# A decoder layer's written order of events: fewer, longer runs of weighings

## What is computed

```python
def _attn(q_in, k_in, v_in, wq, bq, wk, bk, wv, bv, wo, bo, causal):
    Q = (q_in @ wq + bq).reshape(Bq, Sq, H, HD)
    Kp = (k_in @ wk + bk).reshape(Bq, Sk, H, HD)
    V = (v_in @ wv + bv).reshape(Bq, Sk, H, HD)
    scores = jnp.einsum('bqhd,bkhd->bhqk', Q, Kp) / jnp.sqrt(jnp.float32(HD))
    if causal:
        scores = jnp.where(mask, scores, -jnp.inf)
    a = jax.nn.softmax(scores, axis=-1)
    o = jnp.einsum('bhqk,bkhd->bqhd', a, V).reshape(Bq, Sq, Dm)
    return o @ wo + bo
x = _layernorm(x + _attn(x, x, x, sa_wq, sa_bq, sa_wk, sa_bk, sa_wv, sa_bv, sa_wo, sa_bo, True), ln1_g, ln1_b)
x = _layernorm(x + _attn(x, encoder_output, encoder_output, ca_wq, ca_bq, ca_wk, ca_bk, ca_wv, ca_bv, ca_wo, ca_bo, False), ln2_g, ln2_b)
x = _layernorm(x + _moe(x, router_w, router_b, e_w1, e_b1, e_w2, e_b2), ln3_g, ln3_b)
```

## Time and profile before

| | us |
|---|---|
| three runs | 981.31, 982.85, 984.86 |
| their median | 982.85 |
| the profiled execution | 977.55 |
| its span, first to last instruction | 975.8 |
| PE busy in the span | 943.1 |
| DVE busy | 593.7 |
| ACT busy | 557.3 |
| POOL busy | 341.0 |
| matmuls L946 (1,024 of cross, in the page's group) busy | 129.5 |

### The profile page before, as it was taken

How to read it: one execution, slowest core, us unless ns; L and a number is a source line. 1 busy time by engine, 2 the same in 40 slices (tenths; PEclk the granted TensorE clock), 3 DMA queues, 4 the chain that set the end, 5 groups by cost and what they waited for, 6 DMA issues and landing times.

```text
span 975.8 us, 18808 instructions
## 1 busy us (share of the span) xinstructions
PE 943.1 (97%) x5812; PEld 551.2 (56%) x5813; DVE 593.7 (61%) x1006; ACT 557.3 (57%) x1164; POOL 341.0 (35%) x465
## 2 busy tenths in 40 slices
PE   7899999999999999999999999998998999999995
PEld 4456543533445445333543334234898999999974
DVE  4657798788777887787787788863431211212226
ACT  3354566677765656777666766785343444444442
POOL 3465853534325435313446036112441111111115
PEclk9799999999999999999999999998999999999998
DMA  7363323213114111201624022002231344334225
GB/s 218 99 168 81 92 78 97 56 45 92 43 52 115 50 66 34 66 2 41 215 92 149 4 69 64 12 21 62 44 116 39 118 129 124 120 106 140 49 75 199
DMA packets 93899, 84.04 MB, mean 86 GB/s; under 512 B 37638, under 2 KB 87302, under 8 KB 93702
## 3 DMA queue, kind: packets, MB, share of 16 engines
q1 hardware_dynamic: 85436, 63.93, 23.6%
q0 software_dynamic: 5360, 16.82, 5.0%
q10 hardware_dynamic: 3040, 2.49, 1.0%
HBM read 38.63 MB, written 12.63 MB: 53 GB/s over the span
## 4 chain that ended last, share of the span: by engine, by line
PE 87%; PEld 3%; DVE 3%; DMA 2%; POOL 1%; issue 1%; ACT 1%; PEldq 0%; ACTq 0%; POOLq 0%; DVEq 0%
PE o_bank L946 16%; PE a_bank L929 16%; PE v_slot L893 11%; PE v_slot L1433 11%; PE a_bank L1427 9%; PE a_bank L858 6%; PE a_bank L876 4%; PE v_slot L897 4%; PE v_slot L957 3%; PE o_bank L1427 3%; PE v_slot L898 2%; PEld a_bank L1427 1%; DVE max_q L1116 1%; PEld v_slot L1433 1%; DMA b_sa_bk<-in_sa_bk 1%
## 5 line engine op out<-in xcount | busy, mean ns | idle before, releaser
L1062 ACT ACTIVATE probs<-a_bank 128x512 f32<-128x512 f32 (+1 forms) x688 | 360.3, 591 | 143.4 <-PE a_bank L929 138.0
L1116 DVE TENSOR_REDUCE max_q<-v_slot 128x1 f32<-128x1024 f32 (+3 forms) x352 | 397.8, 1169 | 69.6 <-PE v_slot L893 43.6
L929 PE MATMUL a_bank<-q_stack_cross,k_stack_cross 99*128 99x512 bf16 x512 | 162.8, 381 | 0.6 <-ACT probs L1062 0.3
L1439 ACT ACTIVATE hidden<-a_bank,b 128x128 f32<-128x128 f32 x216 | 79.1, 367 | 144.4 <-PE a_bank L1427 132.8
L893 PE MATMUL v_slot<-k_stack_cross,q_stack_cross 96*128 96x512 bf16 x512 | 148.5, 379 | 0.2 <-DVE max_q L1116 0.2
L1433 PE MATMUL v_slot<-stack_or_weights,hidden 128*128 128x256 f32 x576 | 130.3, 379 | 0.0
L946 PE MATMUL o_bank<-probs,v_cross 128*32 128x512 f32 x1024 | 129.5, 601 | 0.0
L1433 PEld LDWEIGHTS v_slot<-stack_or_weights,hidden 128*128 128x128 f32 x576 | 106.7, 190 | 13.0
L1427 PE MATMUL a_bank<-x_col,stack_or_weights 128*128 128x128 f32 x864 | 109.8, 277 | 2.6 <-issue 2.6
L929 PEld LDWEIGHTS a_bank<-q_stack_cross,k_stack_cross 99*128 99x128 bf16 x512 | 45.3, 97 | 118.4 <-ACT probs L1062 67.0
L1427 PEld LDWEIGHTS a_bank<-x_col,stack_or_weights 128*128 128x128 f32 x864 | 105.9, 194 | 4.9 <-issue 3.2
(11 more groups left out here) (215 smaller groups left out, 1084.3 us busy)
## 6 DMA issues: line engine op xcount, KB each, us to landing
k_stack_cross<-parts SPq DMA_DIRECT2D x96, 128.0 KB, 2.4
stack_or_weights<-in_e_w SPq DMA_DIRECT2D x12, 1024.0 KB, 6.5
stack_or_weights<-parts SPq DMA_DIRECT2D x91, 128.0 KB, 2.4
q_stack_cross<-parts SPq DMA_DIRECT2D x48, 128.0 KB, 2.4
inputs<-in_ctxT POOLq DMA_DIRECT2D x4, 1024.0 KB, 6.1
stack_or_weights<-in_e_w SPq DMA_DIRECT2D x8, 512.0 KB, 5.2
x_slots<-slots_in SPq DMA_DIRECT2D x116, 32.0 KB
y_got<-token_out SPq DMA_DIRECT2D x11, 256.0 KB, 8.1
```

The costliest lines, as they stand in the source:

```text
L929: last = nc.tensor.matmul(bank[:, i * cols:(i + 1) * cols], lhs, q_stack[kind][0:KM, G * u + j, q0:S], start=True, stop=True)
L1062: nc.scalar.activation(probs[tile % PB][:, js[0]:js[-1] + 1, q0:S], a_bank[at % AS][:, 0:len(js) * (S - q0)].rearrange("p (j t) -> p j t", ...
L1116: nc.vector.tensor_reduce(most, rows, X, ALU.max, negate=True).then_inc(v_free, 1)
L1439: nc.scalar.activation(hidden[:, f, :], h_bank[f % HB][:, 0:P], ACT.Gelu, bias=b1[:, bass.ds(e * FC + f, 1)]).then_inc(flow.gelu_done, 1)
```

## The change

`STEPS` is another string of the same length with the same number of each letter. The description of the change counts 94 runs of weighings in place of 134; counted on PE, where two weighings belong to one run if no other matmul stands between them, there are 92 in place of 131: 30 of one weighing, 32 of two, 22 of three and 8 of four, before 89, 26, 13 and 3. Nothing else in the kernel differs. Its first line before and after:

```diff
 STEPS = (
-    "aaaaaammmmmmmmmmrmeeameemeeeeewmrmmeemwmemeeemeeweeeweemrmwwwwamemoameememekveewmerkmeememwmeemeemeewwevmmeeememowowwwro"
+    "aaaaaammmmmmmmmmmreeameemeeeewemmeemrmwmeemeemeeewweeemoewwrwwammeameemmeemkeewmerkmmemwmemeeemeoeewweeemmemeeorwwwweosa"
...
```

More of the change, by code:

```diff
@@ L112 @@
 STEPS = (
-    "aaaaaammmmmmmmmmrmeeameemeeeeewmrmmeemwmemeeemeeweeeweemrmwwwwamemoameememekveewmerkmeememwmeemeemeewwevmmeeememowowwwro"
-    "samasseemaeemvesvmmememammsmeeewreesemmememwmeermaeemwwekmmemrwmeemwmeeemwwemeemamemammwemeemwmeemeeoeweeweeemmeommwwrme"
-    "meemeewwammeemwememkmmeewemeemewememeeemsomomeewwsmemeeaeemrsammesemewwemreemeememeaeewemmeeemwsweemvmeewweemermeeweemee"
-    "mwemmeoeewmeemeweememesememeewowwememeemeemeeweemeermeeemwwwweaememmeekmeemwoemeeemewememekmeemwoeemeemsmemeweermmeeewww"
@@ new lines @@
+    "mmaseeesmvmseeaaemmemreemvemsmmswwwweeemmmeeemeemeraememowwwweemmeremeeemeemammewmemammekommvmeemwmemeewwkmmeemmvmemreem"
+    "wwwweemmemeeemamemamemewemeemeemesmomeaemeemewwwemeeemewweemmeeosrmreemeewwemeemeeseeemeswweeemmemeaemeemewwmeeemwweemee"
+    "mresaemewwmeeememeeemeeememeeoemwwwweememevmeemsmeemeeemwrwweoememmeesmeweremmeeaemkmmeewmemeeammekemmewemeeeomewwwemere"
+    "memeemeemeemeemwwweemmoeemwwemeemeemeeemeemewwemmeeewwmeemeemeeremeemvmmeeewowwmmeememeorevemeemeemeewwweeemmemeeeowemee"
@@ new lines @@
+    "msmemwwwememecammkecemeekmemosvemmerewwcwemsemeaemmevmeemeemeemeecwwwmeeremmaemmesaeemmeewwemeemewwemeeememeeemewweemere"
+    "mcmeemeewwswemmoememeewwemeememeeeceeemmemesmevemeewwwreeememeewweememekmeemwoeememesmmeewemeemkewowwmeememeeemremeemeem"
+    "eewwwecemmeemeemewwemeeemreemoeewwemeeememeewwemeemeewwreemeemeemeveemmeewowweemmeemeemeeemeemerewwweeemeomwwceeemseovme"
+    "meewwecemekemcoeeemkeemsmwweceemeseevmemeemeewwwrwmeeememevemeemeecmeewweemmeeewwememecemeemeecemeemeewwwesevmmemeerewes"
@@ L125 @@
+    "eemmeewweemeemeemkmemsoemeemkmecsememwweememeeeowwweemmeemeemeemeeemewrwwemeemeemeeemeemeweemmeewemeemeemeeemwwwemmeemvr"
+    "ememevcmeeewwwomeemekveememvemmeesmeemwoecmeeemkecemeeewwwememreeemeemeecmewweemeecmeemwweeememewwmeeememeemeeemeweeemme"
+    "ewwwemmeermeemecememwmeemeeemeemeemeeweomeeemewwwwemeeemeememeeeceeemcrweeewceeeweeeweoeeeeeeeeweeeweeeweeeweeeweeeweeww"
     "oocccccc")
```

## The result

The median went from 982.45 us (4 runs, 981.31 to 984.86) to 996.93 us (4 runs, 992.63 to 998.08). The ratio of the two groups of runs is 1.0154, with a 95% interval of 1.0123 to 1.0186 (the medians alone give 1.0147). The forecast was 978.7, and its range ended at 984.5. The profiled execution took 997.66 us, 20.1 more than the one before (977.55), so the profiled pair lies further apart than the medians (14.5).

What follows compares the result with a forecast made beforehand. The prediction took PE to bound attention, busy 627.14 of 629.00 us. Its terms, -9.0 - 0.9 + 0.5 + 1.2 + 4.0 = -4.2 us, set against the median of 982.85, gave 978.7 us, range 973.5 to 984.5.

Steps and rivals of the forecast that it cites:

- Runs: Weighing runs on PE in attention: 39 fewer, at 0.23 us lost for each, give -9.0 us, all on the path.
- Denser stretches: Attention between weighing runs: PE waits for DVE and ACT in 16 more dense stretches, a quarter microsecond each, +4.0 us.
- upper bound: Most the denser stretches could cost: time by which runs outlast DVE's two slots, 6.1 us before, 15.2 after, +9.1.
- rival 3: Attention: ACT becomes the bound, as longer runs leave it idle 24.2 us more, 16.1 lost; 990.8 us, chance 0.11.
- rival 2: Attention: covering engines take the gain back, DVE's added idle time of 9.1 us replacing the 4.0; 983.8 us, chance 0.23.
- The first output projection: PE's wait for o_t goes because bias rows and the input addition now lie ahead of the weighings, -0.9 us.
- Maxima to transposition: Units 2 and 4: too little other PE work before the transposed row of maxima, new waits of +1.2 us.
- Last scores: Attention's last stretch without maxima: nine scores in a row instead of seven, at ACT's pace, +0.5 us.
- At nothing: Moved stack projections, rows of maxima, masks and scatters on POOL's and SP's queues: enough cover, so no cost.
- signs of its failure: PE's clock under 1.00 after the start, stack or mask waits, single waits over 2 us, or changed experts' length.

Runs made afterwards that it cites:

- e1: New order with the bias rows (L912) and the addition to the input (L758) put back behind the fourth unit's run of weighings; 992.93 us, ratio 1.0113.

## Why the prediction was wrong, by its steps

- **Runs, -9.0: right.** 131 became 92, the median loss at a run is 0.23 us in both kernels, and the balance closes with it, with light engines too. (There are 192 weighings and not 256; nothing is worked out from that number.)
- **Denser stretches, +4.0 (0 to 9.1): the step that failed.** The mechanism was right, the size not. What belongs to it is 11.7 us: late scores 7.6, less 1.7 for the rows' DMA and 0.5 for the last scores, 5.4; late maxima 5.8, less 1.1 for the stack's DMA, 4.7; late first maxima and projections 1.6. It is over even the upper bound of 9.1. I had counted 16 stretches at a quarter of a microsecond each, and only those with six maxima or more. The profile shows a quarter for each maximum from the third on (the stretch at 552 us has five), and 42 more late scores and 30 more late maxima. Of the late maxima's 7.1 us, 5.3 lie within 3 us behind the end of a run. The upper bound was DVE's idle time alone; ACT's was set aside as rival 3, and both came true at once, in part.
- **What PE's busy share was taken for: failed with it.** I read 627.14 of 629.00 busy as a sign that PE loses almost nothing and used it against rival 2; by start times the old order has late lines of 9.0 us. In the new order PE reads 635.40 of 646.00, 8.7 us more of idle time, while 25.7 us more are lost. The Trainium skill, "Trainium Kernel Development and Optimization", Performance Expectations, says that matmul busy time is a bad metric for how close a kernel is to roofline, because matmuls are pipelined; in this trace it also hid two thirds of the lost time, by those numbers. The rule that tiling doesn't quicken the emptying of PSUM (the Trainium skill, "TensorEngine Tiling (Array Packing)", PSUM Bottleneck), which the prediction weighed against the trace, agrees with the new order: it is 16.6 us behind with the usual emptying, and level (624.6 against 624.9) with lighter emptying.
- **The first output projection, -0.9: wrong in sign.** The wait for o_t at 86 us went as predicted (0.9). But I asked what the moved bias rows release and not what they wait for: ACT makes them behind its exponentials, 2.3 us, and the clock fell behind that.
- **Maxima to transposition, +1.2:** measured +2.2, in 9 places. **Last scores, +0.5:** measured 0.5 (late scores in the last stretch 1.8 against 1.3).
- **At nothing: wrong by 2.8.** I compared distances on PE; the rows' DMA (1.7) and a stack's (1.1) were late on the way through SP and the DMA engines. The rows had a 1 MB load close ahead of them, and the stack's pieces stood in SP's queue right behind another stack's (issues from 541.1 to 549.6 us without a pause).
- **The clock: not in the sum.** 10.6 us at half in attention cost 6.4, the waits inside them included, and the experts' part, 3.0 us longer, has one such stretch more. The prediction named a clock under 1.00 and single waits over 2 us as signs of its failure, and gave them no price.

What stays open: how much of the 14.5 us is the clock's in an average execution. It is 6.4 of 16.6 in the profiled one, and 3.3 to 10.3 in the other kernels with 92 runs; no run held the clock.

## What to carry to other kernels

In this kernel, work that keeps only PE busy was not just cost: spread singly between work that other engines must empty, it gave them time, and merging it took that time away. So before gathering such work, compare the pace of each engine in the stretch that is left (here 0.87 us of PE against 1.13 of DVE for a maximum and two scores), from the first buffer on and not from the worst place. Read small waits from start times, since neither the busy share nor the list of waits showed them here; and ask of each moved step what it waits for on every queue.

## What was not expected of the hardware

**The clock after short stops.** In the fourteen profiles PE's granted clock fell to 0.50 29 times between 60 us and the last weighing. 12 of these began within 4 us behind a place where PE had stood for 1.5 to 2.2 us by the profile's idle time; there were 17 such places, so 5 passed without. The other 17 began within 4 us behind the router's matmuls (L988, 16 matmuls with 8 columns, 1.9 us, with PE counted busy throughout): 1 in 9 routings with the old order and its variants with light engines, 16 in 33 with the others. A stretch at half clock lasted 3.4 us, in one case 6.8, and PE got about half as much done in it (17 matmuls against 34 above). So a wait of 2 us often cost nearer 4 here. In e1, where the stop at 78 us is gone, the fall behind it is gone too; beyond that, that the stops bring the fall is only read from the order of events. Why the old order's routings mostly pass is open.

**A DVE step beside POOL.** The lengthened steps above. The Trainium skill, "GPSIMD Engine Reference", Specifications, has SBUF's interface shared between the two engines, with contention for DVE instructions with two SBUF inputs; the rows agree: 0.60 to 1.15 us against 0.19 to 0.27 with two, and 0.19 in both kernels with one.
